# Turning x on VectorE and spreading the softmax's inverse sums through HBM, in a group-norm attention block

## The reference

```python
def _group_norm(x, scale, bias):
    B, T, C = x.shape
    xg = x.reshape(B, T, GROUPS, C // GROUPS)
    mean = xg.mean(axis=(1, 3), keepdims=True)
    var = xg.var(axis=(1, 3), keepdims=True)
    xg = (xg - mean) * jax.lax.rsqrt(var + EPS)
    return xg.reshape(B, T, C) * scale + bias

def _qkv_attention(qkv):
    bs, length, width = qkv.shape
    ch = width // (3 * N_HEADS)
    q, k, v = jnp.split(qkv, 3, axis=-1)
    scale = 1.0 / np.sqrt(np.sqrt(ch))
    q = (q * scale).reshape(bs * N_HEADS, length, ch)
    k = (k * scale).reshape(bs * N_HEADS, length, ch)
    v = v.reshape(bs * N_HEADS, length, ch)
    weight = jnp.einsum('btc,bsc->bts', q, k)
    weight = jax.nn.softmax(weight.astype(jnp.float32), axis=-1).astype(qkv.dtype)
    a = jnp.einsum('bts,bsc->btc', weight, v)
    return a.reshape(bs, length, -1)

xf = x.reshape(b, -1, c)
h = _group_norm(xf, norm_scale, norm_bias)
qkv = h @ qkv_w + qkv_b
h = _qkv_attention(qkv)
h = h @ proj_w + proj_b
return (xf + h).reshape(b, *spatial, c)
```

## Time and profile before

| | us |
|---|---|
| median of 3 runs | 3426.82 (3425.06 to 3427.06) |
| profiled execution, its own time | 3426.32 |
| its span | 3424.6 |
| TensorE busy (share of the span) | 3355.7 (98%) |
| VectorE busy | 2813.5 (82%) |
| ScalarE busy | 2085.2 (61%) |
| GpSimd busy | 1645.7 (48%) |

### The profile page before, as it was taken

How to read it: one execution, slowest core, us unless ns; L and a number is a source line. 1 busy time by engine, 2 the same in 40 slices (tenths; PEclk the granted TensorE clock), 3 DMA queues, 4 the chain that set the end, 5 groups by cost and what they waited for, 6 DMA issues and landing times.

```text
span 3424.6 us, 67790 instructions
## 1 busy us (share of the span) xinstructions
PE 3355.7 (98%) x24640; PEld 2542.3 (74%) x24640; DVE 2813.5 (82%) x3473; ACT 2085.2 (61%) x3985; POOL 1645.7 (48%) x2762
## 2 busy tenths in 40 slices
PE   5999999999999999999999999999999999999998
PEld 4777777777777777777777777777777777777775
DVE  4888888888888888888888888888888888888886
ACT  4666665665665656656666566666566666665663
POOL 3444454545545444544444445445454544454552
PEclk9999999999999999999999999999999999999999
DMA  3878778777887877878788787877878778787777
GB/s 114 194 182 196 193 189 197 183 197 189 192 194 185 197 189 192 197 185 195 187 196 194 186 197 182 198 191 190 196 184 198 191 189 198 182 196 189 185 188 177
DMA packets 255707, 646.87 MB, mean 189 GB/s; under 512 B 73872, under 2 KB 73872, under 8 KB 255376
## 3 DMA queue, kind: packets, MB, share of 16 engines
q1 hardware_dynamic: 235792, 604.79, 74.6%
q10 hardware_dynamic: 19584, 37.76, 3.1%
HBM read 71.84 MB, written 33.55 MB: 31 GB/s over the span
## 4 chain that ended last, share of the span: by engine, by line
PE 88%; DVE 4%; ACT 4%; issue 1%; SPq 1%; POOL 1%; DMA 0%; DVEq 0%; POOLq 0%; ACTq 0%
PE pv_ps L373 23%; PE s_ps L344 22%; PE c_ps L407 7%; PE c_ps L408 7%; PE c_ps L409 7%; PE c_ps L419 3%; PE c_ps L421 3%; PE c_ps L420 3%; PE c_ps L391 3%; PE c_ps L393 3%; PE c_ps L392 3%; PE pv_ps L355 3%; DVE turned L610 2%; ACT staged L495 2%; ACT probs L475 2%; PE s_ps L440 2%
## 5 line engine op out<-in xcount | busy, mean ns | idle before, releaser
L475 ACT ACTIVATE probs<-s_ps,neg_max 128x1024 f32<-128x1024 f32 x1024 | 1140.9, 1115 | 821.6 <-DVE neg_max L627 818.4
L627 DVE TENSOR_REDUCE neg_max<-s_ps 128x1 f32<-128x1024 f32 x1024 | 1205.3, 1219 | 411.4 <-PE s_ps L344 411.4
L610 DVE STREAM_TRANSPOSE turned<-probs 128x1024 f32<-128x1024 f32 x1024 | 1233.6, 1229 | 89.9 <-ACT probs L475 70.4
L373 PE MATMUL pv_ps<-probs_t,v 128*64 128x256 f32 x8192 | 943.7, 383 | 6.7 <-DMA probs_t<-turned 6.7
L373 PEld LDWEIGHTS pv_ps<-probs_t,v 128*64 128x64 f32 x8192 | 567.4, 137 | 358.4 <-issue 99.7
L407 PE MATMUL c_ps<-h_hi,w_hi 128*128 128x256 f32 x2048 | 602.7, 294 | 16.7 <-ACT staged L490 8.9
L408 PE MATMUL c_ps<-h_lo,w_hi 128*128 128x256 f32 x2048 | 580.1, 283 | 0.0
L409 PE MATMUL c_ps<-h_hi,w_lo 128*128 128x256 f32 x2048 | 579.5, 283 | 0.0
L495 ACT ACTIVATE staged<-c_ps,qk_bias 64x256 f32<-64x256 f32 x1024 | 481.0, 470 | 125.8 <-PE c_ps L409 112.4
L783 POOL COPY inv_wide<-inv_sum 128x256 f32<-128x256 f32 x256 | 101.5, 397 | 817.4 <-PE pv_ps L355 810.0
L407 PEld LDWEIGHTS c_ps<-h_hi,w_hi 128*128 128x128 f32 x2048 | 392.8, 192 | 20.7 <-ACT staged L490 10.7
(11 more groups left out here) (71 smaller groups left out, 5094.8 us busy)
## 6 DMA issues: line engine op xcount, KB each, us to landing
probs_t<-turned SPq DMA_DIRECT2D x4096, 128.0 KB, 2.4
x_res<-in_x SPq DMA_DIRECT2D x128, 256.0 KB, 3.0
result<-x_res ACTq DMA_DIRECT2D x128, 256.0 KB, 3.1
x_next<-in_x SPq DMA_DIRECT2D x120, 256.0 KB, 3.5
probs_t<-in_L_conv_qkv_w ACTq DMA_DIRECT2D x4, 768.0 KB, 9.0
turned<-in_x SPq DMA_DIRECT2D x4, 512.0 KB, 13.0
probs_t<-in_L_conv_proj_w ACTq DMA_DIRECT2D x4, 256.0 KB, 14.0
v_bias<-in_L_conv_qkv_b SPq DMA_DIRECT2D x1, 256.0 KB, 17.0
```

Of the source, the lines that this page charges most:

```text
L373: last = nc.tensor.matmul(pv_ps[side][CH * par:CH * (par + 1), 0, :], v_sb[:, ring_of(i, parity), CH * chunk:CH * (chunk + 1)], p_t[:, par ...
L475: nc.scalar.activation(probs[k % 2][:, :], s_ps[k % 2][:, :], ACT.Exp, bias=neg_max[:, k % 4:k % 4 + 1], accum_out=row_sum[:, (k // HALF) ...
L610: nc.vector.transpose(dst, probs[k % 2][:, :].rearrange("p (k b j) -> p k b j", k=CHUNKS, b=QUADS)).then_inc(probs_turned, 1)
L627: nc.vector.tensor_reduce(neg_max[:, k % 4:k % 4 + 1], s_ps[k % 2][:, :], AX.X, ALU.max, negate=True).then_inc(max_ready, 1)
```

## The change

The inverse goes another way. VectorE turns a 128x32 tile that holds the four inverse columns (`turn_inverse`), ScalarE's queue stores four pieces of 4x32 in a small HBM tensor `inv_rows`, two of them by turns (`keep_inverse`, in the small step six slots after the half began), and loads it four slots later into `inv_wide` with two transfers of 64 partitions, each reading the same two rows for all of them (`spread_inverse`). `scale_attn` takes `inv_wide` as its second operand. `widen_inverse`, L355 and `take_inverse` are gone.

x is loaded in the order that VectorE's 32x32 turning needs: four transfers of 32 partitions, in pieces of 512 bytes, where one transfer of 128 rows stood, and VectorE turns it straight into `xt_sb` (`turn_x`, in the steps where TensorE transposed). L440 and `copy_x` are gone. Channels then stand in another order on the partitions, so the qkv weights' rows and the norm's vectors are loaded in that order too (four transfers where one stood). In the start all weights are split after the statistics, by q, k and v, and not between them; TensorE waits for each part by itself.

```diff
-STAT_SLOTS = [4, 8, 12, 20, 24, 28, 36, 40]
+TURN_STEPS = [4, 8, 12, 20, 24, 28, 36, 40]
-SMALL_BEFORE = {4: 1, 8: 2, 12: 2}
+SMALL_BEFORE = 2
+KEEP_LAG = 6
-SPREAD_LAG = 8
+SPREAD_LAG = 10
...
-        inv_sum = sb("inv_sum", [P, 2, HALF])
-        inv_wide = sb("inv_wide", [P, HALF * CH])
+        inv_sum = sb("inv_sum", [P, Q])
+        inv_turned = sb("inv_turned", [P, Q])
+        inv_wide = sb("inv_wide", [P, 2, P])
+        inv_rows = nc.dram_tensor("inv_rows", [2, HALF, P], F32, kind="Internal").ap()
...
             for n in range(PPB):
-                sp.dma_start(x_start[n], x_t[0, 2 * n:2 * n + 2].rearrange("n t c -> t n c")
-                             ).then_inc(x_start_loaded[n], 16)
+                for z in range(QUADS):
+                    tiles = x_t[0, 2 * n:2 * n + 2, :, P * z:P * (z + 1)].rearrange("n (a i) c -> i (n a) c", i=Q)
+                    sp.dma_start(x_start[n][Q * z:Q * (z + 1), :].rearrange("p (m c) -> p m c", c=P), tiles
+                                 ).then_inc(x_start_loaded[n], 16)
...
             def load_x_tile(b, u):
                 if within(b, BATCHES - 1):
-                    at_least(sp, xt_full, BLOCKS * (b + 1) + u)
-                    sp.dma_start(x_next[:, :], x_t[b + 1, u]).then_inc(xs_loaded, 16)
+                    at_least(sp, xt_turned, BLOCKS * (b + 1) + u)
+                    for z in range(QUADS):
+                        part = x_t[b + 1, u, :, P * z:P * (z + 1)].rearrange("(a i) c -> i a c", i=Q)
+                        sp.dma_start(x_next[Q * z:Q * (z + 1), :].rearrange("p (a c) -> p a c", a=QUADS), part
+                                     ).then_inc(xs_loaded, 16)
...
-            def spread_inverse(b, k):
-                n = (k - SPREAD_LAG) // HALF
-                half, side = 2 * BLOCKS * b + n, n % 2
-                pe.wait_ge(inv_widened, half + 1)
-                at_least(pe, attn_scaled, half - 1)
-                for u in range(2):
-                    last = nc.tensor.transpose(pv_ps[side][:, 1, u * P:(u + 1) * P], inv_wide[:, u * P:(u + 1) * P],
-                                               ident[:, :])
-                last.then_inc(inv_full, 1)
...
             def attend(b, k):
+                at_least(pe, attn_scaled, half - 1)
...
-            def take_inverse(b, k):
-                n = (k - EVAC_LAG) // HALF
-                half, side = 2 * BLOCKS * b + n, n % 2
-                act.wait_ge(pv_done, half + 1)
-                at_least(act, attn_ready, half)
-                nc.scalar.copy(attn[:, :], pv_ps[side][:, 1, :]).then_inc(inv_taken, 1)
+            def keep_inverse(b, k):
+                n = (k - KEEP_LAG) // HALF
+                half = 2 * BLOCKS * b + n
+                act.wait_ge(inv_turned_ready, half + 1)
+                at_least(act, inv_spread, 32 * (half - 1))
+                for a in range(QUADS):
+                    act.dma_start(inv_rows[n % 2, :, Q * a:Q * (a + 1)], inv_turned[Q * a:Q * a + HALF, :]
+                                  ).then_inc(inv_kept, 16)
+
+            def spread_inverse(b, k):
+                n = (k - SPREAD_LAG) // HALF
+                half = 2 * BLOCKS * b + n
+                act.wait_ge(inv_kept, 64 * (half + 1))
+                at_least(act, attn_scaled, half)
+                for r in range(2):
+                    rows = inv_rows[n % 2, r:HALF:2, :].rearrange("(a u) q -> a u q", a=1)
+                    act.dma_start(inv_wide[CH * r:CH * (r + 1), :, :], rows.broadcast_to([CH, 2, P])
+                                  ).then_inc(inv_spread, 16)
...
+            def turn_x(b, u):
...
+                dst = xt_sb[:, u // 2, :, u % 2 * P:(u % 2 + 1) * P].rearrange("p k (a i) -> p k a i", i=Q)
+                nc.vector.transpose(dst, tile.rearrange("p (a k j) -> p k a j", a=QUADS, k=KT)).then_inc(xt_turned, 1)
...
+            def turn_inverse(b, k):
+                half = 2 * BLOCKS * b + k // HALF - 1
+                dve.wait_ge(inv_ready, half + 1)
+                at_least(dve, inv_kept, 64 * half)
+                nc.vector.transpose(inv_turned[:, :], inv_sum[:, :]).then_inc(inv_turned_ready, 1)
...
-                dve.wait_ge(inv_taken, half + 1)
-                nc.vector.tensor_tensor(attn[:, :], pv_ps[side][:, 0, :], attn[:, :], ALU.mult).then_inc(attn_scaled, 1)
+                dve.wait_ge(pv_done, half + 1)
+                dve.wait_ge(inv_spread, 32 * (half + 1))
+                at_least(dve, attn_ready, half)
+                inv = inv_wide[:, :, :].rearrange("p u q -> p (u q)")
+                nc.vector.tensor_tensor(attn[:, :], pv_ps[side][:, :], inv, ALU.mult).then_inc(attn_scaled, 1)
```

More of the change, by code:

```diff
@@ L422, in make_v, with average_groups @@
                 last.then_inc(v_full, 1)
-            def small(b, k):
-                kind, n = small_unit(k)
-                if not small_taken(b, k)[0]:
+            def average_groups(b, k):
+                n = group_product(k)
+                if n is None or not within(b + 1, BATCHES):
                     return
@@ L542, in step @@
                 s = SPB * b + k
-                if k % HALF == EVAC_LAG % HALF and within(s - EVAC_LAG, N_SLOTS):
-                    take_inverse(b, k)
                 if within(s, N_SLOTS):
@@ L552, in step @@
                     stage_qk(b, k, 0)
-                if small_unit(k)[0] == "stats" and within(b + 1, BATCHES):
-                    copy_x(b, k)
                 if k % 16 == 4:
@@ L562, in step @@
                     stage_qk(b, k, 3)
+                if k % HALF == KEEP_LAG % HALF and within(s - KEEP_LAG, N_SLOTS):
+                    keep_inverse(b, k)
+                if k % HALF == SPREAD_LAG % HALF and within(s - SPREAD_LAG, N_SLOTS):
+                    spread_inverse(b, k)
                 if k % 16 == 6:
@@ L656, in step @@
                     scale_attn(b, k)
+                if k % HALF == 0 and within(s - HALF, N_SLOTS):
+                    turn_inverse(b, k)
                 if within(s, N_SLOTS):
@@ L671, in step @@
                 statistics(b, k)
-                if before_start(b) and k in STAT_SLOTS[1::2]:
-                    split_qkv_weights(STAT_SLOTS.index(k) // 2)
                 if before_start(b) and k == GROUP_VAR_SLOT:
+                    scale_bias()
+                    for part in range(3):
+                        split_qkv_weights(part)
                     split_proj_weights()
```

148 lines of the change are left out of this document (64 added, 84 removed).

## The result

| | before | after |
|---|---|---|
| median | 3425.97 us (4 runs, 3425.06 to 3427.06) | 3595.61 us (4 runs, 3591.48 to 3598.27) |
| ratio | | 1.0494, 95% interval 1.0476 to 1.0512 |
| profiled execution: its span, granted clock | 3424.6 us, 0.997 | 3596.0 us, 0.975 |
| TensorE busy, and the rest of the span | 3355.7 and 68.9 us | 3337.1 and 258.9 us |

The change makes the kernel 4.9% slower. The forecast was 3351 us, the range 3315 to 3419.

A forecast was written before the change was run, and what follows sets the result against it. TensorE, busy 98% of the span, was taken as the bound. 3424.6 - 38.4 - 52.8 + 16 = 3349.4 us of span, so 3351 us as median; range 3315 to 3419.

The forecast's parts named there:

- Gain 1: TensorE's pair L355: removing it saves 0.15 us in each of 256 halves, 38.4 us.
- Gain 2: TensorE's four transposes L440: removing them saves 0.44 us each time, 120 times, 52.8 us.
- VectorE's bill: Turning the inverse and x adds 0.77 us to a large step that TensorE finishes 0.59 us sooner.
- the step at k % 16 = 12: VectorE's idle 1.29 us there becomes -0.07 us, cover used up, in four halves of a batch.
- The start: Before the first scores: turning on VectorE, 16 x issues on SyncE for 4; taken as 0, 5 us either way.
- The inverse's way: Through HBM: load lands after 2.5 us, scaling waits 0.4 us; charged 0.25 us x 64 halves, 16 us.
- The slower rival: Inverse's spread lands 3.9 us after issue, VectorE waits 1.8 us each half: 3434 to 3560 us, chance 0.16.
- The queues: Six ScalarE issues make store and SyncE's moves 3.5 us late every second half; turning about 0.1 us, charged nothing.
- The queue rival: The DMA engines or SyncE's queue become the bound: 3366 to 3419 us, chance 0.18.
- the one for the queue: Sign that the prediction is wrong: VectorE's turnings waiting for the moves of probs_t.
- the one for the start: Sign that the prediction is wrong: scores beginning later than 62 us.
- the 3260 named as right: Sign that the prediction is right: TensorE's busy time near 3260 us.

The follow-up runs named there:

- e10: Kernel before with the inverse's way through HBM alone, ScalarE issuing the two spread loads first, then exponentials, store, and keeps last: 3388.7 us.
- e13: e6 with each x tile's four transfers shared, two issued by SyncE and two by ScalarE behind its keeps: 3345.2 us.
- e1: Changed kernel with the result's store issued ahead of the inverse's six transfers on ScalarE: 3454.9 us.
- e4: Changed kernel with ScalarE's small step reordered: two spread loads first, then exponentials, store, and keeps last: 3404.7 us.
- e6: e4 with the residual load moved behind the first four of SyncE's sixteen moves: 3386.6 us.
- e9: Kernel before with six idle transfers per half that nobody needs, issued behind the result's store on ScalarE's queue: 3427.0 us.

## Why the prediction was wrong

**Gain 1** was right: 38.4 us forecast, 37.4 us of span in e10. **Gain 2** was nearly right: e13's span is 3344.4, 80.2 us under before. With the 37.4 us of the pair and the start's 7.3 us, some 50 us are left for the transposes, of 52.8.

**VectorE's bill** was right in the sum. The turning of x takes 0.67 us but the next instruction starts 0.59 us behind it (1731.29 to 1731.88), that of the inverse takes 0.20 us and frees the engine after 0.12 (1701.33 to 1701.45), 0.71 us together where 0.77 were taken:

```profile
L602 DVE STREAM_TRANSPOSE xt_sb<-x_next 128x512 f32<-128x512 f32 x120 | 80.9, 675 | 0.0
L628 DVE STREAM_TRANSPOSE inv_turned<-inv_sum 128x32 f32<-128x32 f32 x256 | 51.6, 201 | 0.1
```

That the step at k % 16 = 12 has no cover left shows in no wait: in e13 all of TensorE's waits for exponentials together are under 10 us (21.4 in the changed kernel).

**The start** was taken as 0 within 5 us and is +7.3 us, in all kernels with x's part (43.83 to 44.4 us against 36.58). The sixteen issues were named, but not priced. By the first scores it is 8.4 us (64.90 against 56.50).

**The inverse's way** was mis-sized:

```profile
L514 ACTq DMA_DIRECT2D inv_wide<-inv_rows x512: 580/619/2308, 101.2 to 3575.7; - x171
...
DMA to landing us min/median/max: 2.6/3.0/5.1
```

```profile
x_next<-in_x SPq DMA_DIRECT2D x480, 64.0 KB, 2.3
```

The load lands 3.0 us after issue, not 2.5, and never under 2.6, so the scaling waits 0.80 us a half and not 0.4. I had taken less than the store's 3.1 us because a load has a quarter of its bytes. For x's loads of 64 KB that holds, they land after 2.3 us; the load that 64 partitions make of the same two rows takes as long as the store of 256 KB. Why isn't tested. The Trainium skill's formula ("DMA: Bandwidth & Descriptors", Anatomy of one DMA), which that section gives for transfers issued by GpSimd, comes to 2.15 us for 64 KB: near x's 2.3 us, and not borne out by the inverse's 3.0. The term was 16 us, and taking the wait away brought 50 net (e1 to e4). The slower rival named this mechanism and started at 3.6 us of landing; a landing of 3.0 us was already over the cover.

**The queues** are the step that failed, a term put at nothing: "Cost about 0.1 us, in the place where the inverse is waited for anyway: nothing in the sum." The path was followed rightly as far as the turning, and every wait on it was found in the trace. Four things were wrong. The lateness was 4.2 us and not 3.5, since a store that stands behind other issues takes 0.62 us to issue instead of 0.34, and SyncE waits 3.35 us for it (1711.21 to 1714.56) instead of 2.61. The sixteen moves took 10.7 us, not 10.0. By the prediction's own sum that is 4.2 + 15/16 of 10.7 + 2.5 = 16.7 us against 15.2 us of reserve, 1.5 us late; the row shows 1.66. That this fits is partly luck: the landing took 3.4 us there and not 2.5 (1715.01 + 10.0 to 1728.40), and the scaling's 1.43 us of waiting had already moved the turning back. And the reserve had been spent to the last 0.1 us, which I charged as nothing although a us beyond it costs VectorE a us in every second half. Then I stopped at the turning: behind it stands `take_proj`, and TensorE stops for its bank, not for the exponentials that have 1.5 us of reserve. That stop holds VectorE's wait ahead of the scaling beside the one ahead of the turning, and it is paid twice, in 145 us of waiting and in busy time: 3337.1 us against 3251.4 in e13 for the same 23616 instructions, 86 us more, 1.4 us for each of the 62 stops, which is an estimate that puts all of it down to them.

**Rivals.** The queue rival (3366 to 3419) was right that SyncE's list becomes the bound, but gave it by packets on the DMA engines. It is worth 41 us (e6 to e13), and only once the late store and the late spread are gone. The prediction had 12.4 and 12.9 us for SyncE's halves with x, beside 12.5 us of TensorE, and drew no loss from it. (The 12.5 was short: the 12.8 us of a half came from one stretch, where 3424.6 less the 57 us of the start over 256 halves is 13.15 us.) The slower rival had the sign, and its mechanism is real, but with the order of the store mended first it was worth 50 us beside 140.7; the larger one stood under the queues at no price. Of the signs listed as "wrong", two came true: the one for the queue, 105.6 us of turnings behind moves, and the one for the start, scores at 64.90 us where 62 was the limit. TensorE's busy time was 77 us over the 3260 named as right, and e13 has 3251.4.

The steps from the changed kernel to e13, in medians: order of the store 140.7, spread first 50.2, SyncE's wait 18.2, x's issues shared 41.4, in all 250.5 us. The sizes hold for this order of steps; the two in the middle lean on e4, whose runs lie 19 us apart. e13 is then 6 us below the forecast: 3349.4 - 16 (no wait for the inverse) + 7.3 (start) = 3340.7 us of span by its sum, 3344.4 measured.

## What to carry to other kernels

An issue delays all that stands behind it on its queue, by 0.3 to 0.6 us here: list what that is, who waits for that, and go on until you reach the engine that bounds the kernel, past the first wait that "just" fits. Put the issue that others wait for first and the one that has a step to spare last, and share issues between two queues by count when one queue has less slack than an issue or two. And where a reserve is used up to a tenth of a us, price the next us of it: here sixteen moves took 10.7 us and not 10.0, and their landing 3.4 us and not 2.5.

## What the runs showed that was not expected

- The issue of a 256 KB transfer took 0.33 to 0.37 us where nothing stood just ahead of it on its queue (store and x_res before the change, medians 0.34 and 0.33) and some 0.6 us behind other issues (store in the changed kernel 0.61, x_res in e6 0.58). The four keeps of 4x32 take 0.32 us each (median) though they stand in a row, the 64 KB loads of the inverse 0.62. Whether the place or the other queue's issues at that moment make the difference wasn't tested.
- Of issuing from several engines the Trainium skill says ("DMA: Bandwidth & Descriptors", Issuing engines are not separate DMA queues) that it saves only the time to initiate a transfer, usually small beside the transfer. Here that time was the whole difference: two x issues of about 0.5 us moved from SyncE to ScalarE gave 41.4 us (e6 to e13) with the same bytes.
- Six more transfers a half, 1536 in all, left the time within its interval (e9) on DMA engines that are busy three quarters of the time.
- A stop of TensorE of 2 to 3 us costs more than itself: behind one of 3.21 us the granted clock was 0.50 for the next 12 products, which started 0.21 us apart instead of 0.12. Over 500 us the granted clock is 0.98 in the changed kernel and 1.00 before.
